# Score steps side by side on TensorE, and a bank shared between two halves, in the first pass of a four-layer kernel

## The chip, the cores and the metric

The kernel runs on one core of one Trainium2 chip. Its time is the device time of one launch in microseconds (us). TensorE (PE) multiplies matrices and writes to PSUM, eight banks of 512 fp32 columns on 128 partitions. VectorE (DVE) and ScalarE (ACT) read PSUM and SBUF. GpSimd (POOL) reads and writes SBUF only. SyncE (SP) issues the loads and stores. Each engine takes its instructions in the order in which they are written, and waits for another engine on semaphores.

## The reference, cut to what matters

There are four layers on 64 batch elements of 128 tokens with 128 channels. The change touches only layer 0, up to the router of its mixture of experts. For one element:

```
n  = layernorm(x)
x  = x + cross_attention(n, ctx, ctx) @ Wo     # 16 heads of 8, 77 keys, bias by relative position, padding mask
n  = layernorm(x)                              # input of the layer's ffn
h  = layernorm(n) * w1 + b1
h  = causal_conv3(h)                           # each channel by itself
q, k, v = split(h @ attn_w)                    # 16 heads of 8, q and k turned by rope
p  = softmax(where(causal, q @ k.T / sqrt(8), -1e30))
n2 = n + (p @ v) @ proj_w
m  = layernorm(n2) * w2 + b2
expert = argmax(m @ router_w)                  # 4 experts; then the experts, outside this pass
x  = x + n2                                    # the experts' part is added later
```

The kernel writes each token's row to a slot that its expert and its rank among the tokens of that expert set.

## The kernel before

The first pass (part_1a) takes the 64 elements one after the other, with up to eight elements in flight at different stages. Each element goes through three chains: x0 is the cross attention, f0 the causal attention, fc the router. The attention of 16 heads is done in two halves of 8 heads (x0a, x0b, f0a, f0b). A half has the steps S (scores on TensorE), add (bias or causal mask, VectorE), max (VectorE), exp (ScalarE), PT (eight transposes of the probabilities), PTc (copy, ScalarE), PV (times the values) and yg (copy). Then come ygT (transposes), rden and y (VectorE), yT, o (output projection) and x (residual).

The order of the work is written out by hand in a string for each engine: PE_A, ACT_A, DVE_A and POOL_A. A word such as f0b.S@3 says that in turn p the engine does step f0b.S for element p - 3. All 64 turns run the same string, so a period of the pass is one turn. The engines' turns need not begin together; only the waits tie them. Every step counts a semaphore up, and a wait names the step and element that it needs.

Four PSUM tensors of two banks each are shared:

- xs holds scores of x0, and beside them (from column SIDE = 308) x0.T, f0.T and v of f0; also q, k, v of x0 and q, k of f0.
- xp is for PT, PV, ygT, yT and o of x0.
- fs holds the causal scores of f0, one half (8 heads of 128 columns) at a time. The router's logits (fc.route, columns 0 to 3) and the ranks (fc.rank, columns 8 to 11) stand in its first bank.
- fp is for PT, PV, ygT, yT and o of f0. Before the change it also takes the router's transpose fc.T.

The scores of heads 0 to 3 use the contraction rows 0 to 31 of TensorE, those of heads 4 to 7 rows 32 to 63, and so on (tile_position=(g0, 0)). Half a so works on rows 0 to 63 and half b on rows 64 to 127. S of x0 has two fp32 matmuls of 308 columns and two bf16 ones for the padding mask; S of f0 has two fp32 matmuls of 512 columns. An fp32 matmul stands in the trace as two records.

On GpSimd, x0.kblk (L552) and f0.kblk (L561) spread the keys of each head over a block, x0.kblk after VectorE's x0.kT (L880) and f0.kblk after f0.qk (L937, L938). The pass also has there the rstd of three layer norms (eps L541 and L542, rstd L545), fc.z (L570, residual) and fc.scatter (L574, the indirect DMA with a memset, L575, behind it). VectorE's x0b.less (L906) subtracts the maxima from half b of x0; it reads prob and the maxima, both in SBUF. f0.qk reads two parts of probf, both in SBUF.

Of the kernel before, what the change touches and what calls it, by code (L numbers as in the profile page):

```python
# [33 lines left out]
BATCH, TOK, DIM = 64, 128, 128  # L34
# [97 lines left out]
def take_turns(steps, chains):  # L132
# [7 lines left out]
F0_BEHIND = 2  # L140
ROUTE_BEHIND = 2
RANK_BEHIND = 2
PE_A = """
    f0.ygT@5 f0.qkv@3 x0.yT@2 f0.yT@5 fc.rank@6 x0.o@2 x0.T f0.o@5 x0.qkv x0a.PT@1 f0a.S@3 fc.T@5 x0a.S f0a.PT@4
    f0b.S@3 x0a.PV@1 x0b.S f0a.PV@4 x0b.PT@1 f0b.PT@4 f0.T@2 fc.route@5 x0b.PV@1 f0b.PV@4 x0.ygT@1
"""
ACT_A = """
    x0a.PTc@2 fc.xT@6 f0b.exp@5 f0a.PTc@5 x0a.yg@2 x0b.exp@2 f0a.yg@5 x0b.PTc@2 f0b.PTc@5 f0.xT@3 x0b.yg@2 f0b.yg@5
    x0a.exp@1 x0.yT@2 f0.yT@5 f0.v@3 x0.xT f0a.exp@4 x0.v
"""  # L150
DVE_A = """
    f0.conv1@4 x0.aggr@1 f0.conv0@4 fc.first@7 x0.rden@3 f0.rden@6 fc.pick@7 x0.y@3 f0.y@6 fc.taken@7 x0.norm@1
    f0.rope@4 f0.qk@4 f0.x@6 x0.x@3 fc.stats@6 fc.slot@7 x0.kT@1 fc.aggr@6 x0b.max@2 fc.slot_i@7 fc.norm@6 x0.qT@1
    f0a.add@4 f0.stats@3 f0.aggr@3 x0a.add@1 f0a.max@4 x0b.less@2 f0.h@3 f0b.add@4 x0b.add@1 f0.norm@3 f0b.max@4
    fc.max@6 x0a.max@1 fc.eq@6 f0.conv2@3 x0.stats
"""
# [219 lines left out]
def part_1a(nc, d, shared):  # L376

    ident, ones, first, slots, total, slot_base, x_mid, rows, minus_half = (shared[k] for k in (
        "ident", "ones", "first", "slots", "total", "slot_base", "x_mid", "rows", "minus_half"))
    moe_in, moe_loads, prep, w_up1, w_dn1, conv1_rows = (shared[k] for k in ("moe_in", "moe_loads", "prep", "w_up1", "w_dn1", "conv1_rows"))  # L380
    PE_L, ACT_L, DVE_L, POOL_L = (Order(text, BATCH) for text in (PE_A, ACT_A, DVE_A, POOL_A))
    NR, NX, NF = 6, 3, 3
    CLEAR_AHEAD = 3
    LAST = BATCH - 1
    with ExitStack() as ctx:
# [57 lines left out]
        xnc = ring(NF, "xnc", [128, DIM])  # L443
        xncT = ring(NF, "xncT", [128, TOK])
# [6 lines left out]
        fs = ctx.enter_context(nc.psum_tensor("fs", [128, 2, BANK], F32))  # L451
        fp = ctx.enter_context(nc.psum_tensor("fp", [128, 2, BANK], F32))
# [8 lines left out]
        pe_done, act_done, dve_done, pool_done = (sem(n) for n in ("pe_done", "act_done", "dve_done", "pool_done"))  # L461
# [129 lines left out]
        def _(act):  # L591
            def xT(p, e, dst, ps, w=None):
                act.wait_ge(pe_done, PE_L.value(f"{p}.T", e))
                if w is None:
                    nc.scalar.copy(dst[:], ps).then_inc(act_done, ACT_L.did(f"{p}.xT", e))
                else:
                    nc.scalar.activation(dst[:], ps, ACT.Identity, scale=ln_col[:, w:w + 1], bias=ln_col[:, w + 1:w + 2]).then_inc(act_done, ACT_L.did(f"{p}.xT", e))  # L597
# [63 lines left out]
                return chain  # L661

            def fc(e):
                xT("fc", e, xncT[e % NF], fp[:, 0, 0:TOK], 2)
                yield

            for dst, src in weight_loads[0::2]:
# [6 lines left out]
            act.wait_ge(weights_in, 16 * len(weight_loads))  # L674
            act.wait_ge(consts_done, N_CONSTS)
            go_through(ACT_L, dict(x0=x0, x0a=x0_half(0), x0b=x0_half(1), f0=f0, f0a=f0_half(0), f0b=f0_half(1), fc=fc))

        @block.tensor
        def _(pe):
# [91 lines left out]
            def f0_half(hf):  # L771
                p = f"f0{'ab'[hf]}"

                def chain(e):
                    s = e % NF
                    if hf == 0:
                        pe.wait_ge(pool_done, POOL_L.value("f0.kblk", e))
                        if e >= 1:
                            pe.wait_ge(dve_done, DVE_L.value("f0b.add", e - 1))
                        if e >= 1 + ROUTE_BEHIND:  # L780
                            pe.wait_ge(dve_done, DVE_L.value("fc.eq", e - 1 - ROUTE_BEHIND))
                        if e >= 1 + RANK_BEHIND:
                            pe.wait_ge(dve_done, DVE_L.value("fc.slot", e - 1 - RANK_BEHIND))
                    else:
                        pe.wait_ge(dve_done, DVE_L.value("f0a.add", e))
                    for b in range(2):
                        g0 = (2 * hf + b) * GROUP * HDIM
                        last = nc.tensor.matmul(fs[:, b, :], qTf[s][g0:g0 + GROUP * HDIM, :], kblkf[s][g0:g0 + GROUP * HDIM, :, :],  # L788
                                                start=True, stop=True, tile_position=(g0, 0))
                    last.then_inc(pe_done, PE_L.did(f"{p}.S", e))  # L790
                    yield
                    pe.wait_ge(act_done, ACT_L.value(f"{p}.exp", e))
                    if hf == 1:
                        pe.wait_ge(act_done, ACT_L.value("f0a.yg", e))
                    elif e >= 1:
                        pe.wait_ge(act_done, ACT_L.value("fc.xT", e - 1))
                    if hf == 0:
                        pe.wait_ge(act_done, ACT_L.value("f0.v", e))
                    for h in range(HALF):
                        last = nc.tensor.transpose(fp[:, h // GROUP, (h % GROUP) * TOK:(h % GROUP + 1) * TOK], probf[s][:, hf, h * TOK:(h + 1) * TOK], ident[:])  # L800
                    last.then_inc(pe_done, PE_L.did(f"{p}.PT", e))
                    yield
                    weigh_values(p, e, fp, TOK, vaugf[s], probTf[s], hf)
                    yield
                return chain

            def fc(e):
                s = e % NF
                pe.wait_ge(dve_done, DVE_L.value("fc.norm", e))
                nc.tensor.transpose(fp[:, 0, 0:TOK], xnc[s][:], ident[:]).then_inc(pe_done, PE_L.did("fc.T", e))  # L810
                yield
                pe.wait_ge(act_done, ACT_L.value("fc.xT", e))
                pe.wait_ge(dve_done, DVE_L.value("f0b.add", min(e + ROUTE_BEHIND, LAST)))
                if e >= 1:
                    pe.wait_ge(dve_done, DVE_L.value("fc.eq", e - 1))
                if e >= 1 + RANK_BEHIND - ROUTE_BEHIND:
                    pe.wait_ge(dve_done, DVE_L.value("fc.slot", e - 1 - RANK_BEHIND + ROUTE_BEHIND))
                nc.tensor.matmul(fs[:, 0, 0:MOE0], xncT[s][:], w_ro0[:], start=True, stop=True).then_inc(pe_done, PE_L.did("fc.route", e))
                yield
                pe.wait_ge(dve_done, DVE_L.value("fc.taken", e))  # L820
                pe.wait_ge(dve_done, DVE_L.value("fc.pick", e))
                pe.wait_ge(dve_done, DVE_L.value("fc.eq", min(e + RANK_BEHIND - ROUTE_BEHIND, LAST)))
                pe.wait_ge(dve_done, DVE_L.value("f0b.add", min(e + RANK_BEHIND, LAST)))
                if e >= 1:
                    pe.wait_ge(dve_done, DVE_L.value("fc.slot", e - 1))
                rank = fs[:, 0, 8:8 + MOE0]
                nc.tensor.matmul(rank, before_bf[:], pick[s][:], start=True, stop=False)
                nc.tensor.matmul(rank, ones_bf[:], base_bf[:], start=False, stop=False)
                nc.tensor.matmul(rank, ones_bf[:], taken[s][:], start=False, stop=True).then_inc(pe_done, PE_L.did("fc.rank", e))
                yield  # L830
# [1612 lines left out]
```

## Time and profile before

| what | value |
|---|---|
| time, median of 3 runs | 3102.59 us (3098.7 to 3110.01) |
| the profiled execution | 3104.64 us, its span 3102.8 us |
| mean granted TensorE clock | 0.958 |
| first pass in the trace | to about 1100 us |
| PE, DVE, ACT, POOL busy, share of the whole span | 90%, 85%, 78%, 32% |
| PE, DVE, ACT, POOL busy from 400 to 800 us | 377.12, 369.92, 357.84, 153.78 us |

A time in a row is counted from the start of the span. In a timeline the first number is the start and the second the length, so the difference of two starts on one engine tells the pace and a start of another engine after an end tells a handover. Two instructions that follow each other without a wait overlap by some hundredths, so a length is a little more than a pace. Busy time is the time in which at least one instruction of the engine runs. TensorE's ends are modelled.

### The profile page before, as it was taken

Reading aid. Unit: us, or ns where it says so; the run is one execution under the profiler, and the core shown is the slowest. Engines: PE = TensorE matmul, PEld = TensorE weight load, DVE = VectorE, ACT = ScalarE, POOL = GpSimd, SP = SyncE. Lnnn points to the kernel's source line nnn. Section 1 sums busy time; section 2 is a strip of 40 time slices with the busy share of each in tenths; the row PEclk is TensorE's granted clock in tenths of the full one; section 3 lists DMA queues with packets and bytes.
Section 4 is the critical chain, followed back from the end, with each engine's and each line's share of the span. In section 5 each row is a group of like instructions: output and inputs, shape, how many; then the busy total and the mean of one; then the engine's idle time right before and its main releaser. Section 6 shows DMA issues by size and latency. Waiting matters only on the chain. (4 is left out here: it accounts for less than half of the span.)

```text
span 3102.8 us, 78311 instructions
## 1 busy us (share of the span) xinstructions
PE 2789.0 (90%) x28313; PEld 1974.0 (64%) x28313; DVE 2625.1 (85%) x6995; ACT 2435.2 (78%) x6105; POOL 999.4 (32%) x1693
## 2 busy tenths in 40 slices
PE   6999999999999859979999998886689999999997
PEld 4666666666666536657777676332667777777776
DVE  4899999999999625549999997698499999999996
ACT  3889988898889625547777775398499999999995
POOL 1333333333333200025555552000024444444441
PEclk8999999999999769989999998899899999999998
DMA  1011111111111011101111110000300000000000
GB/s 49 27 32 52 54 39 34 34 34 34 34 32 31 19 53 42 44 24 33 35 33 34 34 34 17 25 0 0 102 9 16 16 17 16 16 16 16 16 16 9
DMA packets 177631, 91.15 MB, mean 29 GB/s; under 512 B 46340, under 2 KB 174022, under 8 KB 177252
## 3 DMA queue, kind: packets, MB, share of 16 engines
q1 hardware_dynamic: 171716, 76.85, 9.2%
q0 software_dynamic: 4096, 8.40, 0.8%
q8 instruction: 233, 3.82, 0.5%
q14 instruction: 146, 1.19, 0.1%
q10 hardware_dynamic: 1440, 0.90, 0.1%
HBM read 43.73 MB, written 42.36 MB: 28 GB/s over the span
## 5 line engine op out<-in xcount | busy, mean ns | idle before, releaser
L2336 DVE TENSOR_TENSOR th<-tf 128x2048 f32<-128x2048 f32 (+1 forms) x256 | 574.2, 2244 | 6.1 <-ACT cg L2139 6.1
L2168 ACT ACTIVATE th<-th 128x2048 f32<-128x2048 f32 (+1 forms) x256 | 481.4, 1882 | 0.6 <-DVE th L2336 0.6
L652 ACT ACTIVATE probf<-probf,colf 128x128 f32<-128x128 f32 x1024 | 312.2, 390 | 0.0
L2230 PE MATMUL p_rho<-th,late_w_row 128*32 128x128 f32 x8064 | 276.6, 276 | 4.6 <-ACT th L2168 4.5
L2116 POOL TENSOR_SCALAR colf<-colf 128x1 f32<-128x1 f32 x64 | 134.8, 2107 | 441.9 <-DVE colf L2317 441.9
L2230 PEld LDWEIGHTS p_rho<-th,late_w_row 128*32 128x32 f32 x8064 | 208.1, 109 | 29.0 <-ACT th L2168 6.0
L1765 PE MATMUL acc<-xnT_all,wT 128*128 128x512 f32 x384 | 181.3, 625 | 29.6 <-DVE tmax L1957 13.2
L2179 ACT ACTIVATE tl<-tf 128x128 f32<-128x128 f32 x640 | 199.6, 390 | 0.0
L626 ACT COPY probT<-xp 77x1024 f32<-77x1024 f32 x128 | 128.9, 1007 | 49.3 <-PE xp L747 49.3
L952 DVE TENSOR_TENSOR probf<-fs,causal 128x1024 f32<-128x1024 f32 x128 | 155.2, 1213 | 8.2 <-PE fs L788 8.2
L1765 PEld LDWEIGHTS acc<-xnT_all,wT 128*128 128x128 f32 x384 | 73.5, 198 | 135.0 <-issue 83.0
L955 DVE TENSOR_REDUCE colf<-probf 128x8 f32<-128x1024 f32 x128 | 154.8, 1209 | 0.1
L1187 POOL TENSOR_TENSOR col<-col,minus_half 128x1 f32<-128x1 f32 x256 | 146.2, 571 | 21.3
L1441 DVE SCALAR_TENSOR_TENSOR hb<-tb,p_gv 128x512 f32<-128x512 f32 x67 | 46.1, 687 | 123.9 <-ACT tb L1211 91.9
L788 PE MATMUL fs<-kblkf,qTf 32*128 32x512 f32 x512 | 148.0, 655 | 3.0 <-POOL kblkf L561 2.3
L1195 POOL DMA_INDIRECT ya<-rows,slots x64 | 68.4, 1068 | 253.5 <-DMA rows<-yb 243.5
L542 POOL TENSOR_SCALAR col<-col 128x1 f32<-128x1 f32 x64 | 18.1, 283 | 402.4 <-DVE col L853 396.2
L800 PE MATMUL fp<-ident,probf 128*128 128x128 f32 x1024 | 141.5, 283 | 4.1 <-ACT xncT L597 2.4
L747 PE MATMUL xp<-ident,prob 128*77 128x128 f32 x1024 | 141.7, 283 | 2.0 <-ACT prob L617 1.4
L1184 POOL TENSOR_SCALAR col<-col 128x1 f32<-128x1 f32 x256 | 56.7, 222 | 269.1 <-DVE col L1473 192.0
L2119 POOL TENSOR_TENSOR col<-col,minus_half 128x1 f32<-128x1 f32 x64 | 140.3, 2192 | 5.3
L622 ACT ACTIVATE prob<-prob,col 128x77 f32<-128x77 f32 x512 | 134.6, 349 | 6.6 <-DVE col L900 6.6
(437 smaller groups left out, 8501.0 us busy)
## 6 DMA issues: line engine op xcount, KB each, us to landing
rows<-zeros SPq DMA_DIRECT2D x64, 256.0 KB, 2.4
cxT<-in_ctxT SPq DMA_DIRECT2D x128, 38.5 KB, 1.9
xb<-rows SPq DMA_DIRECT2D x67, 64.0 KB, 1.8
rows<-yb SPq DMA_DIRECT2D x67, 64.0 KB, 1.5
x<-in_x SPq DMA_DIRECT2D x64, 64.0 KB, 1.8
x_mid<-x SPq DMA_DIRECT2D x64, 64.0 KB, 1.5
z<-x_mid SPq DMA_DIRECT2D x64, 64.0 KB
x_next<-z SPq DMA_DIRECT2D x64, 64.0 KB, 1.5
```

What stands on the lines that cost most here:

```text
L652: last = nc.scalar.activation(scores, scores, ACT.Exp, bias=colf[s][:, 16 + HALF * hf + h:17 + HALF * hf + h])
L747: last = nc.tensor.transpose(xp[0:KEYS, h // GROUP, (h % GROUP) * TOK:(h % GROUP + 1) * TOK], prob0[s][:, hf, h * KEYS:(h + 1) * KEYS], id ...
L788: last = nc.tensor.matmul(fs[:, b, :], qTf[s][g0:g0 + GROUP * HDIM, :], kblkf[s][g0:g0 + GROUP * HDIM, :, :], start=True, stop=True, tile_ ...
L800: last = nc.tensor.transpose(fp[:, h // GROUP, (h % GROUP) * TOK:(h % GROUP + 1) * TOK], probf[s][:, hf, h * TOK:(h + 1) * TOK], ident[:])
L952: nc.vector.tensor_tensor(scores, fs[:].rearrange("p b (h k) -> p (b h) k", h=GROUP), causal[:].unsqueeze(1).to_broadcast([128, HALF, TOK] ...
L955: nc.vector.tensor_reduce(colf[s][:, 16 + HALF * hf:16 + HALF * (hf + 1)], scores, X_AXIS, ALU.max, negate=True).then_inc(dve_done, DVE_L. ...
L1187: nc.gpsimd.tensor_tensor(col[s][:, 9:10], col[s][:, 8:9], minus_half[:], ALU.pow).then_inc(pool_done, POOL_M.did(f"{p}.rstd", e))
L1765: last = nc.tensor.matmul(acc[n][:, k, :], wT[:, m, k * CH:(k + 1) * CH], xnT_all[:, i * TTILE:(i + 1) * TTILE], start=True, stop=True)
L2168: nc.scalar.activation(b, b, ACT.Tanh).then_inc(act_done, ACT_L.did(f"t{c}.tanh", e))
L2179: last = nc.scalar.activation(tl[r][:, k, :], tf[s][:, FEAT:FEAT + TOK], ACT.Tanh, bias=tf[s][:, CHUNK[-1] + k:CHUNK[-1] + k + 1])
L2230: last = nc.tensor.matmul(p_rho[r][ROWS * b:ROWS * (b + 1), 0:TOK], w_row[:, ROWS - 1 - a:2 * ROWS - 1 - a], tanh[:, k, :], start=(a == 0) ...
L2336: nc.vector.tensor_tensor(th[i % NT][:, 0:shape[1], :], tf[s][:, CHUNK[n]:CHUNK[n + 1]].unsqueeze(2).to_broadcast(shape), tf[s][:, FEAT:FE ...
```

## The change

The strings of all four engines are new. On TensorE f0b.S now stands directly ahead of x0a.S, and f0a.S directly ahead of x0b.S; before, fc.T stood between f0a.S and x0a.S, and x0a.PV between f0b.S and x0b.S. The router's transpose fc.T goes from fp to the second bank of fs. fc.T, fc.route and fc.rank now use fs after the half a of an element's causal scores was read (f0a.add) and ahead of its half b (f0b.S); before, they stood between half b of one element and half a of the next. The waits are changed to fit:

```diff
 PE_A = """
-    f0.ygT@5 f0.qkv@3 x0.yT@2 f0.yT@5 fc.rank@6 x0.o@2 x0.T f0.o@5 x0.qkv x0a.PT@1 f0a.S@3 fc.T@5 x0a.S f0a.PT@4
...
+    x0.ygT@3 fc.route@7 f0.ygT@6 x0.qkv@1 x0.yT@3 f0.yT@6 fc.rank@7 f0.o@6 x0.o@3 f0b.S@5 x0a.S@1 x0a.PT@2 f0a.PT@5
+    x0a.PV@2 f0a.S@4 x0b.S@1 x0b.PT@2 f0.T@3 f0a.PV@5 fc.T@6 f0b.PT@5 f0.qkv@3 x0b.PV@2 f0b.PV@5 x0.T
...
             def fc(e):
-                xT("fc", e, xncT[e % NF], fp[:, 0, 0:TOK], 2)
+                xT("fc", e, xncT[e % NF], fs[:, 1, 0:TOK], 2)
...
                         if e >= 1:
                             pe.wait_ge(dve_done, DVE_L.value("f0b.add", e - 1))
-                        if e >= 1 + ROUTE_BEHIND:
-                            pe.wait_ge(dve_done, DVE_L.value("fc.eq", e - 1 - ROUTE_BEHIND))
-                        if e >= 1 + RANK_BEHIND:
-                            pe.wait_ge(dve_done, DVE_L.value("fc.slot", e - 1 - RANK_BEHIND))
                     else:
                         pe.wait_ge(dve_done, DVE_L.value("f0a.add", e))
+                        if e >= ROUTE_BEHIND:
+                            pe.wait_ge(dve_done, DVE_L.value("fc.eq", e - ROUTE_BEHIND))
+                        if e >= RANK_BEHIND:
+                            pe.wait_ge(dve_done, DVE_L.value("fc.slot", e - RANK_BEHIND))
...
                         pe.wait_ge(act_done, ACT_L.value("f0a.yg", e))
-                    elif e >= 1:
-                        pe.wait_ge(act_done, ACT_L.value("fc.xT", e - 1))
-                    if hf == 0:
+                    else:
+                        if e >= 1:
+                            pe.wait_ge(dve_done, DVE_L.value("f0.x", e - 1))
                         pe.wait_ge(act_done, ACT_L.value("f0.v", e))
...
-                nc.tensor.transpose(fp[:, 0, 0:TOK], xnc[s][:], ident[:]).then_inc(pe_done, PE_L.did("fc.T", e))
+                if e + ROUTE_BEHIND <= LAST:
+                    pe.wait_ge(dve_done, DVE_L.value("f0a.add", e + ROUTE_BEHIND))
+                else:
+                    pe.wait_ge(dve_done, DVE_L.value("f0b.add", LAST))
+                if e >= 1:
+                    pe.wait_ge(act_done, ACT_L.value("fc.xT", e - 1))
+                nc.tensor.transpose(fs[:, 1, 0:TOK], xnc[s][:], ident[:]).then_inc(pe_done, PE_L.did("fc.T", e))
                 yield
                 pe.wait_ge(act_done, ACT_L.value("fc.xT", e))
-                pe.wait_ge(dve_done, DVE_L.value("f0b.add", min(e + ROUTE_BEHIND, LAST)))
...
-                pe.wait_ge(dve_done, DVE_L.value("f0b.add", min(e + RANK_BEHIND, LAST)))
+                if e + RANK_BEHIND <= LAST:
+                    pe.wait_ge(dve_done, DVE_L.value("f0a.add", e + RANK_BEHIND))
+                else:
+                    pe.wait_ge(dve_done, DVE_L.value("f0b.add", LAST))
```

TensorE in the steady part of the pass, before, around the four score steps (L788 is S of f0, L733 with L737 is S of x0, L810 fc.T, L747 and L800 PT, L698 PV):

```order
L747 MATMUL xp<-ident,prob 77x128 x8
L788 MATMUL fs<-kblkf,qTf 128x512 x2
L810 MATMUL fp<-ident,xnc 128x128
L733 MATMUL xs<-kblk,qT 128x308 x2
L737 MATMUL xs<-drop_bf,ones_bf 128x308 x2
L800 MATMUL fp<-ident,probf 128x128 x8
L788 MATMUL fs<-kblkf,qTf 128x512 x2
L698 MATMUL xp<-probT,vaug 32x128 x8
L733 MATMUL xs<-kblk,qT 128x308 x2
L737 MATMUL xs<-drop_bf,ones_bf 128x308 x2
```

And after the change (the first pair is f0b.S with x0a.S, the second f0a.S with x0b.S):

```order
L788 MATMUL fs<-kblkf,qTf 128x512 x2
L733 MATMUL xs<-kblk,qT 128x308 x2
L737 MATMUL xs<-drop_bf,ones_bf 128x308 x2
L747 MATMUL xp<-ident,prob 77x128 x8
L800 MATMUL fp<-ident,probf 128x128 x8
L698 MATMUL xp<-probT,vaug 32x128 x8
L788 MATMUL fs<-kblkf,qTf 128x512 x2
L733 MATMUL xs<-kblk,qT 128x308 x2
L737 MATMUL xs<-drop_bf,ones_bf 128x308 x2
```

Nothing stands between an S of f0 and an S of x0 any more, and the two of a pair work on different rows of TensorE.

VectorE, before, from the rope product to the scatter's norm (L934 f0.rope, L937 and L938 f0.qk, L993 fc.slot, L880 x0.kT):

```order
L934 TENSOR_TENSOR probf<-xs,rope 128x512
L937 TENSOR_TENSOR qTf<-probf 128x128
L938 TENSOR_TENSOR kTf<-probf 128x128
L942 TENSOR_TENSOR h<-fp,h 128x128
L886 TENSOR_TENSOR x<-xp,x 128x128
L850 BN_STATS colc<-h 128x6
L993 SCALAR_TENSOR_TENSOR colc<-fs,pick 128x4
L880 COPY kT<-xs 128x77
L853 BN_AGGR colc<-colc 128x2
L900 TENSOR_REDUCE col<-prob 128x8
L996 CAST slots<-colc 128x1
L857 TENSOR_SCALAR xnc<-h,colc 128x128
```

VectorE, after, from x0.kT on (the lines of this file are eight higher here: L888 x0.kT, L945 and L946 f0.qk, L1001 fc.slot, L914 x0b.less, L861 fc.aggr):

```order
L888 COPY kT<-xs 128x77
L945 TENSOR_TENSOR qTf<-probf 128x128
L946 TENSOR_TENSOR kTf<-probf 128x128
L1001 SCALAR_TENSOR_TENSOR colc<-fs,pick 128x4
L890 TENSOR_SCALAR qT<-xs 128x128
L914 TENSOR_TENSOR prob<-prob,col 128x616
L950 TENSOR_TENSOR h<-fp,h 128x128
L894 TENSOR_TENSOR x<-xp,x 128x128
L858 BN_STATS colc<-h 128x6
L1004 CAST slots<-colc 128x1
L861 BN_AGGR colc<-colc 128x2
```

The copy kT now stands directly ahead of the two additions of f0.qk, and x0b.less two steps behind them.

GpSimd, before, from f0.kblk to the scatter:

```order
L561 TENSOR_TENSOR kblkf<-kTf,ingroup 128x512
L542 TENSOR_SCALAR colc<-colc 128x1
L545 TENSOR_TENSOR colc<-colc,minus_half 128x1
L552 TENSOR_TENSOR kblk<-kT,ingroup 128x308
L574 DMA rows<-xnc,slots 33152x128
L575 MEMSET colc 128x1
L541 TENSOR_SCALAR colf<-colf 128x1
```

GpSimd, after:

```order
L552 TENSOR_TENSOR kblk<-kT,ingroup 128x308
L561 TENSOR_TENSOR kblkf<-kTf,ingroup 128x512
L542 TENSOR_SCALAR colc<-colc 128x1
L545 TENSOR_TENSOR colc<-colc,minus_half 128x1
L570 TENSOR_TENSOR x<-x,h 128x128
L574 DMA rows<-xnc,slots 33152x128
L575 MEMSET colc 128x1
L541 TENSOR_SCALAR colf<-colf 128x1
L542 TENSOR_SCALAR colf<-colf 128x1
L545 TENSOR_TENSOR colf<-colf,minus_half 128x2
```

The two kblk steps now stand next to each other, and the norm of f0 (the last three rows) stands behind fc's norm, fc.z and the scatter.

## Rows read from the trace of the kernel before

**Rows 1.** Busy time by stretch (us, then each engine), one period of the pass.

```profile
560.57:576.39 15.82, 14.97 (x156) 10.56 (x155) 14.71 (x42) 14.23 (x41) 6.09 (x13) 1.00 0.11 34
```

**Rows 2.** Timeline of TensorE in that period: start, length, what, and waits.

```profile
562.44 1.13 PE L788 MATMUL fs<-kblkf,qTf 32*128 32x512 f32 x4
563.50 0.64 PE L698 MATMUL xp<-probT,vaug 77*32 77x128 f32 x16
564.07 0.79 PE L733 MATMUL xs<-kblk,qT 32*128 32x308 f32 x4
...
564.92 0.65 PE L698 MATMUL fp<-probTf,vaugf 128*32 128x128 f32 x16
...
566.43 1.04 PE L800 MATMUL fp<-ident,probf 128*128 128x128 f32 x8
...
571.41 0.27 PE L688 MATMUL xp<-ident,y 128*128 128x128 f32 x1
```

**Rows 3.** Timeline of VectorE in that period.

```profile
560.37 1.21 DVE L952 TENSOR_TENSOR probf<-fs,causal 128x1024 f32<-128x1024 f32 x1
...
561.92 0.77 DVE L896 TENSOR_TENSOR prob<-xs,bias 128x616 f32<-128x616 f32 x1
562.60 1.21 DVE L955 TENSOR_REDUCE colf<-probf 128x8 f32<-128x1024 f32 x1
563.73 0.79 DVE L906 TENSOR_TENSOR prob<-prob,col 128x616 f32<-128x616 f32 x1
564.43 0.34 DVE L857 TENSOR_SCALAR h<-x,colf 128x128 f32<-128x128 f32 x1
...
572.34 0.29 DVE L937 TENSOR_TENSOR qTf<-probf 128x128 f32<-128x128 f32 x1
572.55 0.28 DVE L938 TENSOR_TENSOR kTf<-probf 128x128 f32<-128x128 f32 x1
...
574.04 0.24 DVE L880 COPY kT<-xs 128x77 f32<-128x77 f32 x1 [0.26 <-PE xs L716]
...
575.36 0.71 DVE L857 TENSOR_SCALAR xnc<-h,colc 128x128 f32<-128x128 f32 x1 [0.26 <-POOL colc L545]
```

**Rows 4.** Timeline of GpSimd in that period.

```profile
560.34 1.09 POOL L574 DMA_INDIRECT rows<-xnc,slots  x1 [0.17 <-DVE xnc L857]
561.44 0.12 POOL L575 MEMSET colc<- 128x1 f32 x1
562.09 0.19 POOL L541 TENSOR_SCALAR colf<-colf 128x1 f32<-128x1 f32 x1 [0.53 <-DVE colf L853]
562.34 0.23 POOL L542 TENSOR_SCALAR colf<-colf 128x1 f32<-128x1 f32 x1
562.55 0.44 POOL L570 TENSOR_TENSOR x<-x,h 128x128 f32<-128x128 f32 x1
562.96 0.72 POOL L545 TENSOR_TENSOR colf<-colf,minus_half 128x2 f32<-128x2 f32 x1
...
572.91 1.04 POOL L561 TENSOR_TENSOR kblkf<-kTf,ingroup 128x512 f32<-128x512 f32 x1 [2.11 <-DVE kTf L938]
574.45 0.22 POOL L542 TENSOR_SCALAR colc<-colc 128x1 f32<-128x1 f32 x1 [0.50 <-DVE colc L853]
...
575.29 0.70 POOL L552 TENSOR_TENSOR kblk<-kT,ingroup 128x308 f32<-128x308 f32 x1
```

**Rows 5.** Instructions of line 857 for xnc: least, median, greatest ns; first and last start.

```profile
L857 DVE TENSOR_SCALAR xnc<-h,colc x64: 345/714/715, 98.4 to 1100.3; 128x128 f32<-128x128 f32 x64
```

**Rows 6.** Timeline of VectorE and GpSimd in the last layer.

```profile
2498.74 2.26 DVE L2336 TENSOR_TENSOR th<-tf 128x2048 f32<-128x2048 f32 x1
2498.92 2.17 POOL L2116 TENSOR_SCALAR colf<-colf 128x1 f32<-128x1 f32 x1 [6.68 <-DVE colf L2317]
...
2502.36 0.22 POOL L2116 TENSOR_SCALAR col<-col 128x1 f32<-128x1 f32 x1 [0.62 <-DVE col L2317]
2502.41 2.15 DVE L2336 TENSOR_TENSOR th<-tf 128x1920 f32<-128x1920 f32 x1
```

More of the change, by code:

```diff
@@ L142 @@
 RANK_BEHIND = 2
-PE_A = """
-    f0.ygT@5 f0.qkv@3 x0.yT@2 f0.yT@5 fc.rank@6 x0.o@2 x0.T f0.o@5 x0.qkv x0a.PT@1 f0a.S@3 fc.T@5 x0a.S f0a.PT@4
-    f0b.S@3 x0a.PV@1 x0b.S f0a.PV@4 x0b.PT@1 f0b.PT@4 f0.T@2 fc.route@5 x0b.PV@1 f0b.PV@4 x0.ygT@1
-"""
 ACT_A = """
-    x0a.PTc@2 fc.xT@6 f0b.exp@5 f0a.PTc@5 x0a.yg@2 x0b.exp@2 f0a.yg@5 x0b.PTc@2 f0b.PTc@5 f0.xT@3 x0b.yg@2 f0b.yg@5
-    x0a.exp@1 x0.yT@2 f0.yT@5 f0.v@3 x0.xT f0a.exp@4 x0.v
+    f0a.yg@5 fc.xT@6 x0b.PTc@2 f0b.PTc@5 x0b.yg@2 f0.v@3 f0b.yg@5 x0.xT x0a.exp@1 f0.yT@5 x0.yT@2 x0.v f0a.exp@4
+    x0b.exp@1 x0a.PTc@1 f0a.PTc@4 x0a.yg@1 f0b.exp@4 f0.xT@2
 """
 DVE_A = """
[L152 to L155, printed above, removed]
+    f0.rden@6 fc.pick@7 f0.y@6 fc.taken@7 x0.kT@1 f0.qk@4 fc.slot@7 x0.qT@1 x0b.less@2 f0.x@6 x0.x@3 fc.stats@6
+    fc.slot_i@7 fc.aggr@6 f0.stats@3 f0.aggr@3 f0b.add@5 x0a.add@1 f0b.max@5 fc.norm@6 f0.h@3 f0.norm@3 x0b.add@1
+    f0a.add@4 f0.conv2@3 f0.conv1@3 x0.stats f0.conv0@3 x0.aggr f0a.max@4 x0.norm f0.rope@3 x0a.max@1 x0b.max@1
+    fc.max@6 x0.rden@2 fc.eq@6 x0.y@2 fc.first@6
+"""
+PE_A = """
+    x0.ygT@3 fc.route@7 f0.ygT@6 x0.qkv@1 x0.yT@3 f0.yT@6 fc.rank@7 f0.o@6 x0.o@3 f0b.S@5 x0a.S@1 x0a.PT@2 f0a.PT@5
+    x0a.PV@2 f0a.S@4 x0b.S@1 x0b.PT@2 f0.T@3 f0a.PV@5 fc.T@6 f0b.PT@5 f0.qkv@3 x0b.PV@2 f0b.PV@5 x0.T
 """
 POOL_A = """
-    fc.rstd@6 x0.kblk@1 fc.scatter@7 f0.eps@3 fc.z@6 f0.rstd@3 x0.eps x0.rstd f0.kblk@3 fc.eps@5
+    x0.eps x0.rstd x0.kblk f0.kblk@3 fc.eps@5 fc.rstd@5 fc.z@5 fc.scatter@6 f0.eps@2 f0.rstd@2
 """
```

## The prediction, as put down before the changed kernel ran

> **What bounds the kernel now.** I read the busy time by stretch first. In one period of the first pass (15.82 us) TensorE is busy 14.97 us, VectorE 14.71 and ScalarE 14.23 [rows 1]; the clock column shows 1.00. No engine alone is the bound. All three are within a tenth of the period, so the bound is a ring of waits through them, and a saving on one engine counts only until the next ring is the longest. The pass turns 63 times between the first and the last fc.norm, which start at 98.4 and 1100.3 us [rows 5]. That is 15.90 us a turn, so 0.1 us a turn is worth 6.3 us of the kernel. Nothing outside the pass is changed.
>
> What VectorE needs for itself comes next. Its idle time is 15.82 - 14.71 = 1.11 us. Where it waits it also loses the overlap of two neighbours, about 0.08 us (563.73 + 0.79 - 564.43 [rows 3]), say five times, 0.35 with rounding. One instruction is long by an accident: fc.norm takes 0.715 us where its least is 0.345 [rows 5]. Without waits and without that 0.37, VectorE would take 15.82 - 1.11 - 0.35 - 0.37 = 14.0 us a turn.
>
> **The score pairs on TensorE.** S of f0 holds TensorE for 1.06 us (562.44 to 563.50) and S of x0 for 0.85 (564.07 to 564.92) [rows 2]. In the first, four records of 512 columns go through in 1.06 us, while PT's eight records of 128 columns take 1.04: twice the columns in the same time, so the two row groups do run beside each other. The two halves of f0.S use two row groups and x0.S the two others. In a pair the x0 part can start when the last pass of the f0 part has started, after about half of 1.06, so the pair takes 0.53 + 0.85 = 1.4 us instead of 1.9. That is 0.5 a pair and 1.0 a turn, down to 14.0 us of TensorE. The bounds are nothing saved (the x0 part waits for the f0 part's end) and 0.85 a pair (x0 wholly hidden). I take 0.5, since the rows show starts in order. Moving fc.T, fc.route and fc.rank adds and removes nothing; each keeps its 0.3 us or less.
>
> The Trainium skill, TensorE: Matmul & The Clock Gate, Part 3 (Packing small matmuls — row/col tiling), gives 3.07 times for four row tiles of 512 columns, where the two here show about two times. With its ratio a pair would save a little more than I take, and the result below would not move.
>
> **What comes late next.** A new ring has to be closed through the new order. I name its parts from x0.kT of one turn.
>
> First, GpSimd against VectorE. VectorE now does x0.kT (0.24 us), then the two additions of f0.qk, about 0.16 and 0.37 us after the start of x0.kT (pace 0.21 [rows 3]). GpSimd hears 0.08 us after an end (572.55 + 0.28 to 572.91 [rows 3, 4]), so x0.kblk starts 0.32 after the start of x0.kT: 0.05 us ahead of the second addition. How do such neighbours behave? At 575.29 x0.kblk started 0.07 ahead of fc.norm. It kept its 0.70 us, and fc.norm ended at 576.07, 0.08 after it, having taken twice its time [rows 3 to 5]. With VectorE 0.18 ahead it is the other way about: a GpSimd instruction on one column took 2.17 us and ended as the addition th<-tf did, which reads both inputs from SBUF like f0.qk and x0b.less. With GpSimd 0.05 ahead of th<-tf it took 0.22 us [rows 6]. So who starts first holds, and at 0.05 the row shows GpSimd as first. Then the second addition ends 0.15 us behind x0.kblk, at 1.17 instead of 0.64: 0.53 lost. f0.kblk then starts at 1.25 and runs to 2.29 (1.04 us). x0b.less starts at about 1.44, again behind GpSimd. It ends at 2.29 plus the 0.66 of its own data, 2.95 instead of 1.71 + 0.53 = 2.24: another 0.71. Together 1.24 us a turn, while fc.norm is freed of its 0.37, which is in the 14.0 already. The bounds: if VectorE wins the second addition, only x0b.less waits, for the rest of x0.kblk, about 0.12; if additions are not held at all, 0.
>
> The Trainium skill, SBUF — State Buffer, section Who interferes with whom, says that a VectorE instruction with two SBUF inputs contends with a GpSimd instruction that reads SBUF, and that issue order decides who blocks. The rows of the last layer agree for the one direction (2.17 us); no row before shows an addition held by GpSimd. By the rule 1.24 or 0.12 is lost, without it nothing.
>
> Second, GpSimd's own chain. f0.h now waits for a chain that begins with fc.aggr: 0.17 for fc.aggr, 0.08 handover, 0.84 for eps and rstd (574.45 to 575.29), 0.41 for fc.z, 1.10 for the scatter, 0.12 memset, 0.25 and 0.31 for the two eps, 0.72 rstd, 0.03 back: 4.03 us [rows 4]. VectorE has beside it two small norm steps (0.5), f0b.add and f0b.max (1.13 each, the pace of 562.60 to 563.73), x0a.add (0.68) and fc.norm (0.26): 3.69 [rows 3]. It waits 0.34.
>
> Third, x0.kT waits for TensorE. From f0a.add to x0.kT TensorE has f0a.add's 1.21 us, fc.T (0.3), eight steps that stand before in the stretch 566.43 to 571.41 (4.98 us [rows 2], some 0.45 of it waits), and x0.qkv (0.95): about 7.0. VectorE's own way from f0a.add to x0.kT is about 6.8. It waits 0.2.
>
> The sum of the ring is 14.0 + 1.24 + 0.34 + 0.2 = 15.8 us a turn, which is what it is before. TensorE gains a full microsecond, and VectorE loses it to GpSimd.
>
> **The ends of the pass.** Before, an element's fc.norm comes 5.28 turns behind its x0.norm (place 22 against place 11 of the 39 steps in VectorE's string, five turns on). After it is 5.72 turns (place 20 against 31, six turns on). The pipeline is 0.44 of a turn deeper: 0.44 x 15.8 = 7 us. The turns give 63 x 0.04 = 2.5 back. So the profiled execution's 3104.64 becomes about 3109, and as it lay 2.05 above the median of the runs, the forecast is 3107 us. A shift of 0.5%, 15.5 us, is what can be told from no change.
>
> **The rivals.**
>
> - *VectorE wins the second addition.* For it: the two additions follow each other closely, and 0.05 us is a thin lead. Against it: the row at 2502.36 with the same lead. Then 0.12 is lost instead of 1.24. VectorE's ring is 14.66, and the ring through ScalarE (x0a.exp, f0a.exp, x0b.exp, x0a.PTc, which now stand in line) comes to about the same, since ScalarE is busy 14.23 before. I take 14.75. That is 63 x 1.07 = 67 us less, 7 back for depth: 3102.6 - 60 = 3043 us. Additions that are not held by GpSimd at all give the same within 8 us.
> - *The pair does not overlap.* The x0 part starts only when the f0 part has ended. For it: starts on TensorE are in order, and after each S the rows show about 0.1 us in which the array empties. Against it: the two row groups within one S do overlap [rows 2]. Each pair then takes 1.9. With GpSimd in the way, x0b.S ends at about 8.6 us on the clock of the ring where x0b.add would start at 8.1, so a turn is 0.5 longer, 16.3: 3107 + 32 = 3139 us. This is the slower side. It decides from a pair of more than 1.65 us on. Without GpSimd in the way a turn would be 15.5 and the time about 3090.
>
> **How the numbers follow.** GpSimd first, pairs overlap: 0.50, 3107 us, own range 3091 to 3123 (0.25 us a turn either way); in it faster 0.15, same 0.6, slower 0.25. VectorE first or not held: 0.32, 3043 us. No overlap with GpSimd first: 0.08, 3139; no overlap without it: 0.04, 3090, half of it faster. The rest, 0.06, is shared out. Faster: 0.075 + 0.32 + 0.02 + 0.02 = 0.43. Same: 0.30 + 0.02 + 0.02 = 0.34. Slower: 0.125 + 0.08 + 0.02 = 0.23. The range of 8 in 10 must hold both the first and the second case: 3035 to 3127.
>
> **What would show it.** In the timeline of the new kernel: S of f0 and S of x0 together in 1.4 us. The second addition of f0.qk (0.28 before) at about 0.8, x0b.less (0.79 before) at about 1.5, fc.norm at 0.35. GpSimd's norm of f0 as the releaser of f0.h, by about 0.3. Fewer than 14.2 us of TensorE busy in a period of 15.8. If the second addition stays at 0.28, the second case holds, and the period is under 15. If TensorE's pair takes 1.9, the third holds. A period under 14.6 would say that I have put in a wait that is not there; a granted clock under 1.00 in the steady part would break every number above.

## The result, and the profile after

| kernel | median (lowest to highest) | ratio to before, 95% interval |
|---|---|---|
| before, beside it | 3101.86 us (3098.7 to 3110.01), 4 runs | |
| changed | 3130.71 us (3130.3 to 3131.77), 4 runs | 1.0091 [1.0077, 1.0105] |
| forecast | 3107 us, range 3035 to 3127 | 1.002 |

The kernel is slower by 29 us. The profiled execution took 3130.64 us, its span is 3128.9 us. The mechanism was the one forecast, but the undisturbed turn of the first pass is 16.23 us instead of 15.8, and in nine turns TensorE's granted clock falls for a short while, which was not forecast.

Busy time by stretch, changed kernel, same columns as [rows 1]: one undisturbed turn, a turn in which the clock falls, the low part of that turn, and the steady stretch.

```profile
559.51:575.74 16.23, 13.36 (x155) 10.17 (x154) 15.37 (x42) 14.23 (x41) 6.12 (x13) 1.00 0.11 32
526.40:543.27 16.87, 14.92 (x155) 11.64 (x154) 15.56 (x42) 13.99 (x41) 6.12 (x13) 0.90 0.11 31
528.25:531.65 3.40, 3.13 (x15) 3.17 (x16) 3.37 (x9) 1.77 (x3) 2.43 (x6) 0.56 0.07 19
400.00:800.00 400.00, 333.24 (x3781) 254.94 (x3773) 376.05 (x997) 346.17 (x976) 147.76 (x290) 0.98 0.13 34
```

TensorE's busy time in a turn fell from 14.97 us [rows 1] to 13.36, more than forecast. VectorE's rose from 14.71 to 15.37, and it now bounds the turn together with what it waits for. The clock column is new too: 0.98 instead of 1.00 in the steady stretch.

TensorE's timeline at the start of the first pair (f0b.S with x0a.S) and around the second (f0a.S with x0b.S), to set beside [rows 2]:

```profile
559.54 0.70 PE L788 MATMUL fs<-kblkf,qTf 32*128 32x512 f32 x2
559.69 0.79 PE L733 MATMUL xs<-kblk,qT 32*128 32x308 f32 x4
...
564.36 0.70 PE L788 MATMUL fs<-kblkf,qTf 32*128 32x512 f32 x2
564.38 0.79 PE L733 MATMUL xs<-kblk,qT 32*128 32x308 f32 x4
564.90 0.59 PE L788 MATMUL fs<-kblkf,qTf 32*128 32x512 f32 x2
565.00 0.30 PE L737 MATMUL xs<-drop_bf,ones_bf 1*128 1x308 bf16 x2
565.42 1.10 PE L747 MATMUL xp<-ident,prob 128*77 128x128 f32 x8
```

In the second pair S of x0 starts 0.02 us after S of f0, while two of the four records of f0 are still to come. The next step starts at 565.42, so the pair holds TensorE for 1.06 us: what S of f0 alone took before. In the first pair (the first two rows) S of x0 starts 0.15 us after S of f0, and the last record ends 1.13 us after the start of the pair.

VectorE's timeline, to set beside [rows 3]. The first rows are fc.aggr, fc.norm and f0.h. Then come f0.rope (L942), x0.kT, the second addition of f0.qk and x0b.less. The first addition starts at 574.53:

```profile
561.71 0.18 DVE L861 BATCH_NORM_AGGREGATE colc<-colc 128x2 f32<-128x6 f32 x1
...
565.15 0.33 DVE L865 TENSOR_SCALAR xnc<-h,colc 128x128 f32<-128x128 f32 x1
566.10 0.34 DVE L865 TENSOR_SCALAR h<-x,colf 128x128 f32<-128x128 f32 x1 [0.62 <-POOL colf L545]
...
571.19 0.69 DVE L942 TENSOR_TENSOR probf<-xs,rope 128x512 f32<-128x512 f32 x1 [0.17 <-PE xs L767]
...
574.38 0.23 DVE L888 COPY kT<-xs 128x77 f32<-128x77 f32 x1
...
574.73 0.81 DVE L946 TENSOR_TENSOR kTf<-probf 128x128 f32<-128x128 f32 x1
...
575.74 1.57 DVE L914 TENSOR_TENSOR prob<-prob,col 128x616 f32<-128x616 f32 x1
```

GpSimd's timeline, to set beside [rows 4]:

```profile
561.98 0.22 POOL L542 TENSOR_SCALAR colc<-colc 128x1 f32<-128x1 f32 x1 [1.56 <-DVE colc L861]
...
562.82 0.46 POOL L570 TENSOR_TENSOR x<-x,h 128x128 f32<-128x128 f32 x1
563.45 1.09 POOL L574 DMA_INDIRECT rows<-xnc,slots  x1 [0.16 <-DVE probf L960]
564.54 0.12 POOL L575 MEMSET colc<- 128x1 f32 x1
564.75 0.19 POOL L541 TENSOR_SCALAR colf<-colf 128x1 f32<-128x1 f32 x1
...
565.31 0.75 POOL L545 TENSOR_TENSOR colf<-colf,minus_half 128x2 f32<-128x2 f32 x1
...
574.69 0.70 POOL L552 TENSOR_TENSOR kblk<-kT,ingroup 128x308 f32<-128x308 f32 x1 [4.07 <-DVE kT L888]
575.62 1.04 POOL L561 TENSOR_TENSOR kblkf<-kTf,ingroup 128x512 f32<-128x512 f32 x1 [0.23 <-DVE colc L1001]
```

Read the last two fences together. x0.kblk starts at 574.69, 0.04 us ahead of the second addition of f0.qk. The addition takes 0.81 us instead of the 0.28 of [rows 3] and ends at 575.54, 0.15 after x0.kblk. f0.kblk starts 0.12 ahead of x0b.less. That ends at 577.31, which is f0.kblk's end at 576.66 and 0.65 more; alone it takes 0.79. So a held instruction ends nearly as if it had begun at the holder's end, some 0.14 us earlier than that: the addition, too, ends 0.15 behind its holder and takes 0.28 alone. Over the whole pass (least, median, greatest in ns), with fc.norm to set beside [rows 5]:

```profile
L946 DVE TENSOR_TENSOR kTf<-probf x64: 282/810/814, 63.4 to 1092.4; 128x128 f32<-128x128 f32 x64
L914 DVE TENSOR_TENSOR prob<-prob,col x64: 944/1568/1651, 30.1 to 1062.2; 128x616 f32<-128x616 f32 x64
L865 DVE TENSOR_SCALAR xnc<-h,colc x64: 334/335/478, 105.2 to 1126.8; 128x128 f32<-128x128 f32 x64
```

By these lengths VectorE loses (0.81 - 0.28) + (1.57 - 0.79) = 1.31 us a turn to GpSimd. The last fc.norm starts 26.5 us later than in [rows 5], and the profiled execution is 26.0 us longer, so the loss lies in the first pass.

### The profile page after: what moved, and what is told of

It reads as the page before. It is cut to its first block and busy times, and to the rows that moved or that the text cites. A ratio compares the mean times of both kernels' runs of the same rounds, so it can differ in the third digit from the quotient of the medians.

```text
span 3128.9 us, 78312 instructions
## 1 busy us (share of the span) xinstructions
PE 2708.6 (87%) x28313; PEld 1964.4 (63%) x28313; DVE 2670.7 (85%) x6995; ACT 2431.7 (78%) x6105; POOL 1002.2 (32%) x1693
## 5 line engine op out<-in xcount | busy, mean ns | idle before, releaser
L652 ACT ACTIVATE probf<-probf,colf 128x128 f32<-128x128 f32 x1024 | 313.4, 394 | 16.9 <-DVE colf L963 16.9
L747 PEld LDWEIGHTS xp<-ident,prob 128*77 128x77 f32 x1024 | 121.9, 158 | 126.0 <-ACT probf L652 80.6
L747 PE MATMUL xp<-ident,prob 128*77 128x128 f32 x1024 | 152.0, 296 | 55.3 <-ACT probf L652 52.6
L800 PE MATMUL fp<-ident,probf 128*128 128x128 f32 x1024 | 148.2, 292 | 8.4 <-ACT ygf L659 5.6
L788 PE MATMUL fs<-kblkf,qTf 32*128 32x512 f32 x512 | 148.1, 655 | 0.0
L656 ACT COPY probTf<-fp 128x1024 f32<-128x1024 f32 x128 | 129.5, 1011 | 17.9 <-PE fp L800 17.9
L1192 POOL TENSOR_SCALAR col<-col 128x1 f32<-128x1 f32 x256 | 56.8, 222 | 268.9 <-DVE col L1481 191.8
```

What stands on the lines that cost most here:

```text
L652: last = nc.scalar.activation(scores, scores, ACT.Exp, bias=colf[s][:, 16 + HALF * hf + h:17 + HALF * hf + h])
L747: last = nc.tensor.transpose(xp[0:KEYS, h // GROUP, (h % GROUP) * TOK:(h % GROUP + 1) * TOK], prob0[s][:, hf, h * KEYS:(h + 1) * KEYS], id ...
```

## The experiments

All change the order strings of the changed kernel and nothing else, so each computes the same. Two theories are set against each other. A: VectorE bounds the turn, through the two held additions and the wait for GpSimd's chain before f0.h. B: TensorE or the deeper pipeline bounds it. The kernel before took 3102.83 us beside the first four and 3101.65 beside the others.

### 1. f0.qk ahead of x0.kT

```diff
-... x0.kT@1 f0.qk@4 fc.slot@7 ...
+... f0.qk@4 x0.kT@1 fc.slot@7 ...
```

> The changed kernel with one swap in VectorE's order: f0.qk now stands ahead of x0.kT, so x0.kblk on GpSimd cannot start while f0.qk is under way. Theory A (GpSimd holds VectorE's two-input additions, and that is on the ring): the second addition falls from 0.81 to 0.28 us; x0b.less is held by the rest of x0.kblk alone and falls from 1.57 to about 1.2; the turn goes from 16.23 to 15.1 to 15.3 us and the time to 3131 - 63 x 1.0 = 3065 us (3055 to 3080). If f0.kblk gets ahead of x0b.less again, x0b.less stays above 1.5 and only 0.5 a turn is won, 3100 us. Theory B (the turn is set by TensorE's side: fc.T, fc.route and fc.rank between the halves of the causal scores, and the score pairs): VectorE's waits take up what is freed, and the time stays at 3131 us within 8.

Measured: 3073.08 us (3069.32 to 3077.15), ratio 0.9905 [0.9888, 0.9921]. VectorE and then GpSimd in this kernel, in one turn and on to the next x0.kblk:

```profile
505.35 0.34 DVE L865 TENSOR_SCALAR h<-x,colf 128x128 f32<-128x128 f32 x1 [0.62 <-POOL colf L545]
...
513.82 0.28 DVE L946 TENSOR_TENSOR kTf<-probf 128x128 f32<-128x128 f32 x1
...
514.52 1.17 DVE L914 TENSOR_TENSOR prob<-prob,col 128x616 f32<-128x616 f32 x1
```

```profile
514.33 0.70 POOL L552 TENSOR_TENSOR kblk<-kT,ingroup 128x308 f32<-128x308 f32 x1 [4.46 <-DVE kT L888]
514.99 1.59 POOL L561 TENSOR_TENSOR kblkf<-kTf,ingroup 128x512 f32<-128x512 f32 x1
...
529.70 0.70 POOL L552 TENSOR_TENSOR kblk<-kT,ingroup 128x308 f32<-128x308 f32 x1 [4.46 <-DVE kT L888]
```

The turn is 529.70 - 514.33 = 15.37 us, 0.86 less than in the changed kernel. The second addition is back at 0.28 and x0b.less is held for 0.38 instead of 0.78: 0.93 us less in all. So the held additions stand on the path that sets the turn, and their price is close to what their lengths say. The 0.38 go with x0.kblk, which starts 0.19 ahead of x0b.less. The holding turns round as well: f0.kblk starts 0.47 after x0b.less and takes 1.59 us instead of 1.04. The wait of 0.62 before f0.h stays. The clock does not fall between 140 and 1000 us here, so of the 58 us won some 54 are the shorter turn (63 x 0.86) and the rest is about what the nine falls cost.

### 2. The scatter behind the norm of f0

```diff
-... fc.z@5 fc.scatter@6 f0.eps@2 f0.rstd@2
+... fc.z@5 f0.eps@2 f0.rstd@2 fc.scatter@6
```

> The changed kernel with one step moved in GpSimd's order: fc.scatter stands behind f0.eps and f0.rstd instead of ahead of them. Theory A: f0.h, which waits 0.62 us for GpSimd's norm, waits no more; the way from fc.aggr to f0.h falls from 4.39 to VectorE's own 3.7, the turn from 16.23 to about 15.5 us, the time to 3131 - 63 x 0.7 = 3087 us (3080 to 3097). Theory B: 3131 us within 8.

Measured: 3118.56 us (3113.55 to 3119.92), ratio 1.0049 [1.0032, 1.0065]. GpSimd's timeline from one x0.kblk to the next, and VectorE's from f0.h on:

```profile
500.94 0.70 POOL L552 TENSOR_TENSOR kblk<-kT,ingroup 128x308 f32<-128x308 f32 x1 [3.91 <-DVE kT L888]
...
507.31 1.09 POOL L574 DMA_INDIRECT rows<-xnc,slots  x1 [0.18 <-issue]
...
516.67 0.70 POOL L552 TENSOR_TENSOR kblk<-kT,ingroup 128x308 f32<-128x308 f32 x1 [3.92 <-DVE kT L888]
```

```profile
507.88 0.55 DVE L865 TENSOR_SCALAR h<-x,colf 128x128 f32<-128x128 f32 x1
508.13 0.36 DVE L865 TENSOR_SCALAR xnf<-x,colf 128x128 f32<-128x128 f32 x1
...
510.57 0.29 DVE L933 TENSOR_SCALAR hcT<-xnTf,conv_col 128x128 f32<-128x128 f32 x1 [0.25 <-ACT xnTf L597]
```

This turn is 15.73 us, 0.50 less than 16.23: the chain of GpSimd ahead of f0.h stands on the path too. From fc.aggr (504.19) to f0.h it is now 3.69 us instead of 4.39, as expected. Of these 0.70 us, 0.2 come back: VectorE now waits 0.25 for ScalarE's xnTf ahead of f0.conv2 (hcT, L933), where it did not wait in the changed kernel's turn. That f0.h runs beside the scatter and takes 0.55 us instead of 0.34 costs nothing, since the next instruction starts 0.25 after it, as before. The total missed the expectation by some 30 us. About 13 of them are the turn (15.73 where 15.5 was expected). In 18 stretches of 3.4 us TensorE's granted clock stood at the lower level, 1.2 GHz, and turns with such a stretch took 16.7 to 16.9 us (one 17.3). That is some 20 us, where the nine such stretches of the changed kernel cost about 5. The kernel before has none between 140 and 1000 us.

### 3. The pairs taken apart

```diff
-... f0.o@6 x0.o@3 f0b.S@5 x0a.S@1 ... x0a.PV@2 f0a.S@4 x0b.S@1 ...
+... f0.o@6 f0b.S@5 x0.o@3 x0a.S@1 ... f0a.S@4 x0a.PV@2 x0b.S@1 ...
```

> The changed kernel with both pairs of score steps taken apart again on TensorE: x0.o stands between f0b.S and x0a.S, and x0a.PV between f0a.S and x0b.S; nothing else moves. Theory A: the score steps have over 1 us of slack ahead of x0b.add, so the turn stays at 16.23 us and the time at 3131 us within 6, though TensorE is busy about 0.9 us a turn longer. Theory B (TensorE sets the turn): 0.9 us a turn is lost, 3131 + 57 = 3188 us.

Measured: 3186.59 us (3183.72 to 3190.56), ratio 1.0271 [1.0254, 1.0288]. Busy time by stretch, two turns that follow each other:

```profile
566.81:584.71 17.90, 16.77 (x154) 11.88 (x154) 15.57 (x42) 14.11 (x42) 6.13 (x13) 0.90 0.10 29
584.71:600.97 16.26, 15.24 (x154) 10.69 (x154) 15.46 (x42) 14.00 (x42) 6.12 (x13) 1.00 0.11 33
```

Where the clock is full, the turn is 16.26 us as expected: the 15.24 - 13.36 = 1.9 us that the pairs save TensorE are worth nothing while VectorE bounds the turn. The loss is in the other turns. TensorE and VectorE in the first of them:

```profile
569.70 1.99 PE L747 MATMUL xp<-ident,prob 128*77 128x128 f32 x8
```

```profile
575.32 0.80 DVE L904 TENSOR_TENSOR prob<-xs,bias 128x616 f32<-128x616 f32 x1 [1.27 <-PE xs L737]
```

PT of x0 (L747) takes 1.99 us instead of 1.10, and VectorE waits 1.27 for the scores. There are 24 such stretches, 22 of 3.4 us and two of 13.7. So this order costs its time through the clock, and neither theory had the clock in it. That the total is the one theory B foretold (3188 us) is chance: the turn at full clock is theory A's.

### 4. f0.qk first, x0b.less away from GpSimd, the scatter behind

```diff
-... x0.kT@1 f0.qk@4 fc.slot@7 x0.qT@1 x0b.less@2 f0.x@6 ... fc.max@6 x0.rden@2 ...
+... f0.qk@4 x0.kT@1 fc.slot@7 x0.qT@1 f0.x@6 ... fc.max@6 x0b.less@1 x0.rden@2 ...
```

The edit of experiment 2 on GpSimd comes with it.

> The changed kernel with three moves: f0.qk ahead of x0.kT, x0b.less directly behind x0b.max and fc.max where GpSimd has nothing large to do, and fc.scatter behind f0.rstd. Theory A: no addition is held (0.28 and 0.79 us), f0.h does not wait for GpSimd, and VectorE's own 14.0 us and its few handovers set the turn: 14.6 to 14.9 us, the time 3131 - 63 x 1.45 = 3040 us (3030 to 3055), faster than both kernels. Theory B: 3131 us within 10.

Measured: 3072.28 us (3071.51 to 3077.5), ratio 0.9902 [0.9886, 0.9919]. A miss of some 30 us: the turn is 15.33. Both additions run unheld (medians 0.282 and 0.799 us), and yet the kernel gains nothing over the first experiment. VectorE's waits from 400 to 800 us, as sum, times and longest:

```profile
DVE prob L904 <- PE fs L788: 9.4, 25, 1.3
DVE h L950 <- PE fp L691: 6.8, 24, 0.3
```

x0b.less now stands ahead of x0.rden and x0.y. The waits fit this chain: y comes late, then the output projection and the pair behind it, and these keep VectorE's own next additions waiting, 16 us in 400. The next experiment leaves x0b.less where it was and has a turn 0.45 us shorter, so the move of x0b.less is what cost the time; the way through TensorE is read from the waits.

### 5. f0.qk first and the scatter behind

The edits of experiments 1 and 2 together, x0b.less left in its place.

> The changed kernel with two moves together: f0.qk ahead of x0.kT, and fc.scatter behind f0.rstd; x0b.less stays where the change put it. Each alone took the undisturbed turn from 16.23 to 15.38 and 15.73. Theory A (one ring through VectorE and GpSimd, whose terms add): 16.23 - 0.85 - 0.50 = 14.9 us, the ring through y, yT and o that bound the three-move kernel at 15.33 is shorter here by x0b.less (0.7) and does not bind: time 3131 - 63 x 1.35 = 3046 us (3035 to 3060), faster than the kernel before. Rival: another ring at about 15.3 us binds already, whatever VectorE does; then 3072 us as with either of the earlier kernels.

Measured: 3040.91 us (3035.41 to 3047.57), ratio 0.9809 [0.9782, 0.9836]. It beats both kernels, by 61 and 90 us. Its steady stretch by engine, and GpSimd's timeline from one scatter to the next:

```profile
400.00:800.00 400.00, 358.53 (x4125) 269.80 (x4124) 389.25 (x1101) 371.36 (x1074) 177.61 (x322) 1.00 0.14 35
```

```profile
500.34 1.09 POOL L574 DMA_INDIRECT rows<-xnc,slots  x1 [0.18 <-issue]
...
510.77 1.60 POOL L561 TENSOR_TENSOR kblkf<-kTf,ingroup 128x512 f32<-128x512 f32 x1
...
515.22 1.09 POOL L574 DMA_INDIRECT rows<-xnc,slots  x1 [0.18 <-issue]
```

The turn is 14.88 us. TensorE's granted clock does not fall between 140 and 990 us. The two savings add up: 0.86 + 0.50 = 1.36, and 16.23 - 1.36 = 14.87. VectorE is busy 97% of the stretch, held time counted as busy.

### 6. The same, with the pairs apart

The edit of experiment 3 on the kernel of experiment 5.

> The kernel with the two moves (f0.qk ahead of x0.kT, fc.scatter behind f0.rstd), and both score pairs taken apart on TensorE as before (x0.o between f0b.S and x0a.S, x0a.PV between f0a.S and x0b.S). It asks what the pairs are worth once the turn is short. If TensorE is then near the ring, 0.7 to 0.9 us a turn is lost, turn 15.6, time 3046 + 50 = 3096 us. If pairs are worth nothing there too, it stays within 10 us of its twin. A falling clock would come on top: turns over 1 us longer than their neighbours.

Measured: 3181.24 us (3168.12 to 3187.72), ratio 1.0261 [1.0232, 1.0291]: 140 us more than with the pairs and 85 more than expected. A turn at full clock and VectorE's longest waits:

```profile
567.84:584.46 16.62, 15.01 (x155) 10.63 (x155) 14.72 (x44) 13.99 (x42) 6.61 (x13) 1.00 0.11 32
```

```profile
DVE prob L904 <- PE xs L737: 23.1, 24, 2.0
DVE hcT L933 <- ACT xnTf L597: 16.8, 23, 0.9
DVE x L894 <- PE xp L691: 11.4, 23, 0.7
```

Here the paired order has a direct worth: 16.62 - 14.88 = 1.74 us a turn at full clock, close to the 2 times 0.85 that the two steps of x0 take when they run alone. VectorE now waits for the scores and for the output projection, so with GpSimd out of its way a ring through TensorE binds next. The edit also puts x0.o and x0a.PV one step later, and the waits of the third row are for x0.o; how much of the 1.74 is that and how much the lost overlap, no run separates. Nineteen stretches at the lower clock come on top, in turns of 17.7 us.

### 7 and 8. One pair apart at a time

On the changed kernel, first the pair f0b.S x0a.S alone, then the pair f0a.S x0b.S alone.

> The changed kernel with only the first pair taken apart (x0.o between f0b.S and x0a.S). With both apart the undisturbed turns stayed at 16.27 us, and every second one took 17.88, in which TensorE's clock was granted at half for 3.4 us. Theory C (all the loss is the clock): undisturbed turns 16.2 to 16.3; the time is 3131 us plus what the dips cost, so 3131 to 3160. Rival (a ring through the score step): undisturbed turns of 16.6 us or more.

> The changed kernel with only the second pair taken apart (x0a.PV between f0a.S and x0b.S). Theory C: undisturbed turns 16.2 to 16.3 us, and dips of the clock to half tell the rest: 3131 to 3160 us. Rival (a ring through x0b.S and x0b.add): undisturbed turns of 16.6 us or more. Whichever of this and the kernel with the first pair apart shows the dips, tells which gap on TensorE goes with them.

Measured: 3177.57 us (3177.11 to 3178.04), ratio 1.0243 [1.0209, 1.0276], and 3140.13 us (3136.2 to 3144.06), ratio 1.0122 [1.0086, 1.0158]. Two turns in a row of the first:

```profile
544.40:560.64 16.24, 14.43 (x154) 10.39 (x154) 15.39 (x42) 14.23 (x41) 6.13 (x13) 1.00 0.11 32
560.64:577.77 17.13, 15.99 (x154) 11.97 (x154) 15.57 (x42) 13.99 (x41) 6.12 (x13) 0.90 0.11 31
```

Both have 16.24 us in a turn at full clock, as the changed kernel has, so all the loss is in turns with a fall, as theory C says. But the first, at 3178 us, lies above the 3160 that was the most expected. It has 34 stretches at the lower clock (27 of 3.4 us, seven of 6.8) and the second nine, like the changed kernel. In the second such a turn is 17.6 us instead of 16.8, perhaps because TensorE has less slack to take it up; nine times 0.8 is most of the 9 us that it is slower. Of the two edits, then, only the one at f0b.S and x0a.S brings more falls. It also puts x0.o behind f0b.S, and it gives more falls alone (34) than with the other edit (24), so that it is the pair itself that keeps the clock up is not shown. Each count is of one profiled execution.

## Why the prediction was wrong

- *The bound.* Right. A ring through three engines, and a saving on TensorE that VectorE does not pass on. TensorE saved 1.6 us of busy time a turn and the turn grew.
- *The score pairs.* The direction right, the size too small: 1.06 us instead of 1.4. The reason given, that the x0 part starts only when the last pass of f0 has started, is refuted by the 0.02 us between the two starts in the second pair and the 0.15 in the first. It moved nothing at full clock, as TensorE did not bound (experiment 3). The rival in which the pair does not overlap is excluded by the same row.
- *VectorE's own need, 14.0 us.* Right. Counted from start to start, the undisturbed turn holds 0.53 + 0.79 us for the two held additions, 0.69 for the wait ahead of f0.h and 0.24 for the one ahead of f0.rope: 16.23 - 2.25 = 13.98.
- *GpSimd against VectorE.* Right in mechanism, in who wins, and in size: from the start of x0.kT to the end of x0b.less it is 2.93 us, forecast 2.95. From start to start the loss is 1.32 us instead of 1.24. Experiment 1 shows it by taking it away.
- *GpSimd's chain ahead of f0.h: the step that failed.* It was put at 4.03 us and measures 4.39, from the start of fc.aggr at 561.71 to that of f0.h at 566.10. From fc.z to the scatter are 0.63 us and not 0.41, since 0.16 of idle stand ahead of the indirect DMA. The same idle stands in the row before (0.17 ahead of 560.34 [rows 4]), but there fc.norm ended only 0.09 ahead of the scatter, so the row could be read as a wait for it; experiments 2 and 5, with 0.18 and nothing waited for, decide. From the memset to f0.eps are 0.21, not 0.12. The wait of f0.h is 0.62 instead of 0.34. Experiment 2 shows that the chain is on the path.
- *x0.kT waits for TensorE, 0.2 us.* It does not wait, but f0.rope, 3.2 us earlier, waits 0.17 for TensorE. From f0a.add to x0.kT it is 7.05 us (567.33 to 574.38), put at 7.0.
- *The sum.* Piece by piece, against the forecast: fc.aggr to f0.h 4.39 (4.03), f0a.add to x0.kT 7.05 (7.0), and the other two pieces, x0.kT to fc.aggr and f0.h to f0a.add, 3.56 + 1.23 = 4.79 (4.75, what is left of the forecast's 15.78). That is 16.23 instead of 15.78 us, and 0.36 of the 0.45 are the one chain. In the forecast's own terms the wait for it is 0.28 too small. Another 0.14 is the overlap that VectorE loses at its two waits, 0.07 each: the forecast took such losses off VectorE's need and did not put them back for the waits that it added. The holds are 0.08 more, the need and the wait for TensorE together 0.05 less.
- *The ends of the pass.* Put at 7 us. The first fc.norm starts 105.2 - 98.4 = 6.8 later. Right for the start. But the last five turns, as the pipeline runs out, were not in the sum. Before they took 81.8 us, 2.7 more than five steady ones, with the clock at the lower level from 1048 us on; after they took 74.6, 6.6 less than five steady ones.
- *The clock.* The forecast took 1.00 as given. Nine turns have such a stretch; eight of them are 0.5 to 0.7 us longer than 16.23, so it costs about 5 us (the ninth, 17.77 us, stands where the kernel before has two long turns, too). It is the second thing missing. The miss is smaller than the two together: 63 x 0.45 = 28 and 5 make 33 us, and from the first fc.norm to the last the forecast is 22 short (1021.6 instead of 999.4 us). The last five turns gave back 9, so without that luck the miss would have been larger.
- *The rival at 3043 us.* It was excluded by the 0.81 us of the second addition. But it was also priced too low: experiment 1 takes 0.93 of the 1.32 us of holding away and stands at 3073, because GpSimd's chain is still there. It takes both to come to 3041.

Why the clock falls at all stays open. The rows give no answer by busy time or by idleness of TensorE. The changed kernel has TensorE busy 83% from 400 to 800 us and the clock falls nine times over the pass, experiment 3 has 94% and 24 falls, the kernel before has 94% and none between 140 and 1000 us, and experiment 5 has 90% and none before 990 us. TensorE's wait does not tell either. These are the transposes L747 just after a fall (first row) and in an undisturbed turn, with the same wait ahead:

```profile
528.52 1.86 PE L747 MATMUL xp<-ident,prob 128*77 128x128 f32 x8 [0.95 <-ACT probf L652]
```

```profile
561.62 1.07 PE L747 MATMUL xp<-ident,prob 128*77 128x128 f32 x8 [0.95 <-ACT probf L652]
```

## What to carry to other kernels

When two instructions that were seen to hold each other, one on VectorE and one on GpSimd, come to start within some tenths of a microsecond, work out who is first to a few hundredths, and try the neighbour order: an exchange of two words in VectorE's string was worth 58 us here. When a step is put behind another engine's chain, add the idle time between that chain's instructions, not only their lengths, and mind that an indirect DMA in the chain costs its issue (1.09 us here, and 0.16 ahead of it) to everyone behind it. Where a wait is added to a sum, add the lost overlap of its neighbours as well, 0.07 us here. And a saving that shows no worth while another engine bounds the turn can carry a large one once that bound is lifted: the paired order was worth nothing at full clock in the changed kernel and 1.74 us a turn in the best one.

## What the runs showed of the hardware

- Four row groups of TensorE worked at once: S of f0 and S of x0 in 1.06 us, against 1.06 + 0.85 one after the other [rows 2]. In the second pair the second step's first record starts 0.02 us after the first step's, ahead of the first step's last records.
- Held instructions go both ways, and a held one ends some 0.14 us before it would have if it had begun at the end of the holder: x0b.less 1.57 us instead of 0.79 behind f0.kblk, f0.kblk 1.60 instead of 1.04 behind x0b.less. In the changed kernel x0.kblk starts 0.03 to 0.04 us ahead of the second addition in 61 of 64 turns, and in 60 of them the addition is held (0.81 us).
- A GpSimd indirect DMA has 0.16 to 0.18 us of idle ahead of it also where nothing is waited for (the rows of experiment 5 say "issue"). A VectorE scale-and-shift that starts beside it took 0.55 us instead of 0.34, and the next instruction started no later for it (0.25 us after).
- Within a pass whose turns are all alike, the granted clock of TensorE fell to 1.2 GHz, mostly for stretches of 3.4 us, and came back to 2.4, as often as 34 times between 140 and 1000 us, and differently often in orders of the same instructions. It fell never in experiment 1, once in experiment 4, nine times in the changed kernel and in experiment 8, and 18, 19, 24 and 34 times in experiments 2, 6, 3 and 7.
